# Last stage of a fused transformer kernel: a floor written as a reduction, a rotation in one instruction, and a new order of the pieces

## What is computed

```python
for i in range(6):
    x = attn_layer(shift_tokens(x), Wqkv[i], q_scale[i], k_scale[i], Wo[i]) + x
    x = ffn_layer(shift_tokens(x), ln_g[i], ln_b[i], W1[i], b1[i], W2[i], b2[i]) + x

def attn_layer(x, Wqkv, qs, ksc, Wo):          # 16 heads of 64
    q, k, v = jnp.split(x @ Wqkv, 3, -1)       # then split in heads
    q, k = l2norm(q) * qs, l2norm(k) * ksc     # l2norm: t / max(norm(t), 1e-12)
    q = q * cos * scale + rotate_half(q) * sin * scale
    k = k * cos / scale + rotate_half(k) * sin / scale
    out = local_attention(q, k, v)             # windows of 32, each sees itself and the one before, softmax
    return out @ Wo                            # heads joined again

def ffn_layer(x, g, bln, W1, b1, W2, b2):      # 341 wide
    a, gate = jnp.split((layernorm(x) * g + bln) @ W1 + b1, 2, -1)
    return a * gelu(gate) @ W2 + b2
```

## Time and profile before

| | us |
|---|---|
| median of 3 runs | 2295.93 |
| lowest and highest | 2290.71, 2298.35 |
| the profiled execution | 2290.53 |
| its span in the trace | 2288.7 |

### The profile page before, as it was taken

How to read it: one execution, slowest core, us unless ns; L and a number is a source line. 1 busy time by engine, 2 the same in 40 slices (tenths; PEclk the granted TensorE clock), 3 DMA queues, 4 the chain that set the end, 5 groups by cost and what they waited for, 6 DMA issues and landing times. The chain is left out here.

```text
span 2288.7 us, 52278 instructions
## 1 busy us (share of the span) xinstructions
PE 1844.2 (81%) x18512; PEld 917.1 (40%) x18512; DVE 1718.1 (75%) x3041; ACT 1279.6 (56%) x1850; POOL 922.8 (40%) x913
## 2 busy tenths in 40 slices
PE   5655888888888888888855888988988987988886
PEld 3531222222222222222222655655655655655554
DVE  4744777777677777777737988978988988987984
ACT  4411666656666666666644656655655655655653
POOL 0002111111111111111016877766776776775770
PEclk9955999999899999999978999999999999999998
DMA  1002223232323232322004333323332332332330
GB/s 34 1 17 62 54 57 61 57 60 56 60 56 60 56 60 56 60 56 57 2 3 130 94 95 94 95 87 89 93 94 76 95 105 76 95 105 67 95 85 10
DMA packets 88745, 152.83 MB, mean 67 GB/s; under 512 B 16819, under 2 KB 51669, under 8 KB 84693
## 3 DMA queue, kind: packets, MB, share of 16 engines
q1 hardware_dynamic: 86421, 149.04, 26.6%
q10 hardware_dynamic: 2112, 0.94, 0.2%
HBM read 98.03 MB, written 51.12 MB: 65 GB/s over the span
## 5 line engine op out<-in xcount | busy, mean ns | idle before, releaser
L899 DVE TENSOR_REDUCE ENM<-PM 128x1 f32<-128x512 f32 x1024 | 658.5, 686 | 249.9 <-PE PM L722 240.9
L819 ACT ACTIVATE EPT<-PA 128x1024 f32<-128x1024 f32 x512 | 512.3, 1021 | 219.3 <-PE PA L734 139.3
L722 PE MATMUL PM<-EKX,EQX 48*128 48x512 bf16 x1024 | 354.3, 399 | 103.1 <-DVE ENM L899 83.7
L1293 POOL TENSOR_TENSOR DRN<-DRN,DHALF 128x8 f32<-128x8 f32 x192 | 352.2, 1835 | 8.7
L1291 POOL TENSOR_TENSOR DQR<-DR 128x512 f32<-128x512 f32 x192 | 254.3, 1324 | 245.5 <-DVE DR L1581 221.2
L642 POOL CAST ENMP<-ENM 128x16 bf16<-128x16 f32 x64 | 12.7, 198 | 781.2 <-DVE ENM L899 781.2
L744 PE MATMUL PV<-EPT,EVP 128*32 128x512 f32 x2048 | 283.1, 626 | 0.9 <-ACT EPT L819 0.7
L722 PEld LDWEIGHTS PM<-EKX,EQX 48*128 48x128 bf16 x1024 | 85.5, 94 | 477.6 <-DVE ENM L899 392.5
L734 PE MATMUL PA<-EQX,EKX 51*128 51x512 bf16 x1024 | 253.2, 394 | 28.2 <-DMA EQX<-EROWS 14.2
L1337 PE MATMUL PM<-DWQKV,DXS 128*128 128x512 f32 x384 | 213.3, 638 | 38.3 <-ACT DRAW L1499 24.7
L1499 ACT ACTIVATE DRAW<-PM 128x512 f32<-128x512 f32 x192 | 114.9, 598 | 156.4 <-DVE DR L1581 93.1
(11 more groups left out here) (208 smaller groups left out, 2937.4 us busy)
## 6 DMA issues: line engine op xcount, KB each, us to landing
DV<-d_vpark SPq DMA_DIRECT2D x192, 256.0 KB, 5.1
d_vpark<-DVT SPq DMA_DIRECT2D x48, 512.0 KB, 2.6
e_park<-EPARTS SPq DMA_DIRECT2D x64, 192.0 KB, 2.9
EQX<-e_park SPq DMA_DIRECT2D x32, 384.0 KB, 5.4
EKX<-e_park SPq DMA_DIRECT2D x32, 384.0 KB, 9.1
DWQKV<-in_WqkvR SPq DMA_DIRECT2D x6, 1536.0 KB, 8.6
e_park<-EPARTS SPq DMA_DIRECT2D x64, 128.0 KB, 2.7
e_park<-EPARTS SPq DMA_DIRECT2D x64, 64.0 KB, 2.1
```

Source lines behind the costliest of these rows:

```text
L722: pe.matmul(PM[:, r, :], lhsT=QX[64 * r:64 * r + KQ, b, hp, t * 128:(t + 1) * 128], rhs=KX[64 * r:64 * r + KQ, b, hp, :], start=True, stop ...
L819: s_.activation(PT[:, kt, pair * 2 * S:(pair + 1) * 2 * S], PA[:, 2 * pair:2 * pair + 2, :].rearrange("p a b -> p (a b)"), ACT.Exp, scale= ...
L899: v.tensor_reduce(NM[:, g % 2, t, j, 0:1], PM[:, r, :], AX.X, ALU.max, negate=True).then_inc(maxed, 1)
L1293: g.tensor_tensor(rn, rn, HALF[:, 0:8], ALU.pow).then_inc(rooted.sem, 1)
```

## The change

- The floor: the sums get a second column that is set to 1e-24 once, and the floor becomes a maximum over the two columns with `tensor_reduce` in place of a `tensor_scalar`.
- The second product of the rotation is one `tensor_tensor` of 512 elements that reads the halves of each head in swapped order (a step of -1 over the two halves), in place of two of 256.
- The places are new. POOL's and SP's lists stay as they were. What changes in the lists (a prime marks a piece of the layer before):
  - DVE: `score` of tile n comes ahead of `weigh` of tile n-1, where it came behind it. `f1b` comes behind p1 (it came ahead of p0), `f1c` still between p2 and the next piece. The second `f3v` comes behind p1 (it came ahead of it). In round 8 `score` 7 and `weigh` 6 come behind `f4`, in the next turn of the loop, where they came ahead of the loop's end on either side of it.
  - PE: `f1b` comes behind p2 (it came right behind `f1a`, ahead of p1); the first `f3` ahead of `mix`; `score` 7 ahead of the loop's end, where it was the first piece of the loop.
  - ACT: `f1a` behind p0 in place of ahead of it; `exp` ahead of the third `f3`, where it came behind it: f33, f34, exp1, f35 in round 3 and f30, f31, exp6, f32 in round 8.

```diff
 TILE_PLACES = {
-    "score": {"tensor": (2, 4), "vector": (1, 48)},
-    "exp": {"scalar": (3, 2)},
-    "weigh": {"vector": (2, 45)},
-    "pturn": {"tensor": (3, 5), "scalar": (3, 7)},
-    "mix": {"tensor": (3, 25), "vector": (3, 17)},
-    "oturn": {"tensor": (3, 39), "scalar": (3, 32)},
-    "out": {"tensor": (3, 42), "vector": (3, 36)},
+    "score": {"tensor": (1, 49), "vector": (2, 0)},
+    "exp": {"scalar": (2, 44)},
+    "weigh": {"vector": (3, 8)},
+    "pturn": {"tensor": (3, 1), "scalar": (3, 8)},
+    "mix": {"tensor": (3, 28), "vector": (3, 12)},
+    "oturn": {"tensor": (3, 36), "scalar": (3, 35)},
+    "out": {"tensor": (3, 44), "vector": (3, 34)},
 }
 BATCH_PLACES = {
-    ("shift", None): {"tensor": (0, 4), "scalar": (0, 4), "gpsimd": (0, 4)},
-    ("f1a", None): {"tensor": (7, 12), "scalar": (7, 6)},
-    ("f1b", None): {"tensor": (7, 17), "vector": (7, 4), "gpsimd": (7, 26)},
-    ("f1c", None): {"vector": (7, 31.5)},
-    ("f2", None): {"tensor": (8, 14), "scalar": (8, 11)},
-    ("f3", 0): {"tensor": (8, 27), "scalar": (8, 26)},
-    ("f3", 1): {"tensor": (8, 37), "scalar": (8, 31)},
-    ("f3", 2): {"tensor": (8, 40.5), "scalar": (8, 45.5)},
-    ("f3v", 0): {"vector": (8, 0)},
-    ("f3v", 1): {"vector": (8, 20)},
-    ("f3v", 2): {"vector": (8, 34.5)},
-    ("f4", None): {"tensor": (8, 49), "vector": (8, 45)},
+    ("shift", None): {"tensor": (0, 0), "scalar": (0, 0), "gpsimd": (0, 0)},
+    ("f1a", None): {"tensor": (7, 11), "scalar": (7, 14)},
+    ("f1b", None): {"tensor": (7, 33), "vector": (7, 28), "gpsimd": (7, 26)},
+    ("f1c", None): {"vector": (7, 30.5)},
+    ("f2", None): {"tensor": (8, 13), "scalar": (8, 14)},
+    ("f3", 0): {"tensor": (8, 26), "scalar": (8, 23)},
+    ("f3", 1): {"tensor": (8, 35), "scalar": (8, 32)},
+    ("f3", 2): {"tensor": (8, 40.5), "scalar": (8, 44.5)},
+    ("f3v", 0): {"vector": (8, 9)},
+    ("f3v", 1): {"vector": (8, 23)},
+    ("f3v", 2): {"vector": (8, 30.5)},
+    ("f4", None): {"tensor": (8, 48), "vector": (8, 48)},
 }
...
-        SS, RN = m.sb("DSS", [128, 2, 8]), m.sb("DRN", [128, 2, 32])
+        SS, RN = m.sb("DSS", [128, 2, 8, 2]), m.sb("DRN", [128, 2, 32])
...
+                chain.link(v.memset(SS[:, :, :, 1], 1e-24))
...
-                        v.tensor_tensor(r2[:, :, 0:32], x[:, :, 32:64], bc(tab[:, 1, 0:32], 1, [128, 8, 32]), ALU.mult).then_inc(step, 1)
-                        v.tensor_tensor(r2[:, :, 32:64], x[:, :, 0:32], bc(tab[:, 1, 32:64], 1, [128, 8, 32]), ALU.mult).then_inc(rotated.sem, 1)
+                        halves = lambda y: y.rearrange("p h (s e) -> p h s e", s=2)
+                        v.tensor_tensor(halves(r2), halves(x)[:, :, ::-1, :], bc(tab[:, 1].rearrange("p (s e) -> p s e", s=2), 1, [128, 8, 2, 32]),
+                                        ALU.mult).then_inc(rotated.sem, 1)
                         wait(squared, k)
-                        v.tensor_reduce(SS[:, k % 2, :], SQ[:, k % 2, :].rearrange("p (h e) -> p h e", h=8), AX.X, ALU.add).then_inc(summed.sem, 1)
+                        v.tensor_reduce(SS[:, k % 2, :, 0], SQ[:, k % 2, :].rearrange("p (h e) -> p h e", h=8), AX.X, ALU.add).then_inc(summed.sem, 1)
                         wait(summed, k)
-                        v.tensor_scalar(RN[:, n[0] % 2, 8 * c:8 * c + 8], SS[:, k % 2, :], 1e-24, None, ALU.max).then_inc(floored.sem, 1)
+                        v.tensor_reduce(RN[:, n[0] % 2, 8 * c:8 * c + 8], SS[:, k % 2, :, :], AX.X, ALU.max).then_inc(floored.sem, 1)
```

## The result

The changed kernel takes 2286.45 us (median of 20 runs, 2276.71 to 2295.86), the kernel before 2299.21 us beside it (20 runs). The ratio is 0.9942, 95% interval 0.9924 to 0.996: 13 us faster, where 39 to 41 had been forecast. The profiled execution has a span of 2281.7 us, 7.0 less than before. What is read from traces is therefore always a stretch within the stack.

A forecast was written before the change was run, and what follows sets the result against it. DVE was taken to set the pace in the middle rounds, and chains in rounds 7 and 8. Terms -20 - 12.5 - 18 + 12 + 0 = -38.5 us gave 2252.0 or 2257.4, called 2255 us; range 2212 to 2292.

The forecast's parts named there:

- Middle rounds: Rounds 4 to 6 and two like them in the first layer: 1.0 us gained each, 20 us in all, bounds 6 and 38.
- Score ahead of weigh: DVE's swapped order in the middle rounds: costs nothing, as PE's score ends 1.4 us before DVE comes to it.
- the walk through the round: Middle round, piece by piece: floor gains kept 0.5 at p0, 0.1 p1, 0.2 p2, 0.3 to 0.5 p3, rotation 4 x 0.07.
- The floor: DVE's floor as a reduction: about 0.17 us, free of POOL's block, so DVE reaches its next instruction about 0.55 us sooner.
- POOL's work stays: POOL will be at its addition or multiplication in most of the time DVE gains; the block at p3 remains.
- The rotation: One product of 512 elements on DVE for two: 0.07 us saved a piece, or 0.55 lost if swapped reads ran half rate.
- Rounds 0 to 2: POOL is the next bound, f1c's wait goes: 2.5 us gained, five times, 12.5 us, bounds 0 and 25.
- Round 7: DVE's 1.04 us wait before f1c goes and three pieces shorten: 3.0 us gained, six times, 18 us, bounds 9 and 27.
- Round 3: ACT's exp and two loads before the third gelu, 3.62 us: 2.4 us lost, five times, 12 us, bounds 0 and 22.
- rival 3: Table switches delay the third gelu and PE's clock falls while it waits: slower, up to 6 us a place, 2308 us; chance 0.11.
- Round 8 and the loop's end: PE's f4 slips about 2.4 us, but the loop-end pauses are hidden: 0, six times, bounds 6 gained and 14 lost.
- Rival 1: POOL takes the gain: DVE's wait at the floor moves to L1579; 12 us gained in all, 2281 us; chance 0.22.

The follow-up runs named there:

- its own kernel: The kernel before with only the second product of the rotation put in one instruction: 2307.36 us against 2310.31, ratio 0.9991.
- f1 places alone: The kernel before with only the new places of f1a and f1b: 2289.79 us, ratio 0.9943.
- forms alone: The kernel before with the new instructions (floor as a reduction, rotation in one) and the old places: 2288.93 us, ratio 0.9949.
- places alone: The kernel before with all the new places and the old instructions: 2313.95 us, ratio 1.0067.
- exp behind: The kernel after, but with exp on ACT behind the third gelu again: 2258.11 us, ratio to the kernel before 0.9821.

## Why the prediction was wrong, point by point

The way was right, the size was not: 13 us gained in place of 39 to 41. The measured 2286.45 us lie within the range that the rivals had widened to 2212 to 2292, and outside the forecast's own bounds of 2228 to 2278.

- **Middle rounds.** 1.0 us each forecast, 1.2 measured, but the nearness is partly luck. The forms, from which all of the 1.0 was to come, gave 0.7 alone. Score ahead of weigh was said to cost nothing and was given no gain; it is 0.5 us a round. The floor fell to 0.17 us without spread, and p2 and p3 stay blocked, as the walk through the round had it.
- **The floor.** The step "POOL's work stays" held: 37% of the freed time returned at the first product.
- **The rotation.** 0.07 us a piece was forecast and no difference was measured; its own kernel won 0.5 us in three middle rounds and lost 1.3 in round 2.
- **Rounds 0 to 2.** 2.5 us forecast. 0.8 were gained from the first product to the first score, and 1.6 in round 2 when the `weigh` that left it is counted: 2.4. The 1.5 of the f1 places alone say the same of round 2.
- **Round 7.** 3.0 forecast and measured. The reason held as far as the traces go: a wait gone and shorter pieces. `f1c`'s wait for POOL is gone with the places (idle 2.8 us in all ahead of it, 14.2 before) and not with the forms alone (16.4). With the forms alone round 7 takes 24.2 us in the mean (23.0 in two of the four layers), with the places alone 24.4, and with both 21.9: it takes both. How the 3.0 us divide into the two was not measured apart from the clock, which differs between these traces.
- **Round 3: the term that was mis-sized.** 2.4 us forecast, 4.6 measured, 4.2 of it gone with exp behind. The parts were named: load, exp and load 3.66 us, `f3v` late, 1.3 us for the score. What was left out of the sum is the clock: PE, idle for 2.6 us, took 4.48 to 5.49 us for `f4` in all five layers, and not the 2.94 of before, 2.0 us more in the mean. The prediction has this in rival 3 and not in the forecast.
- **Round 8 and the loop's end: the step that failed.** I let a slip of 2.4 us and a hidden pause at the loop's end cancel. The slip was about right: `f4` starts 3.0 us later after its score when the moved `weigh` is taken off, and 2.2 of that go with exp behind. The pause was not hidden: the stretch from `f4` to the next layer's first product took 15.15 us before and 15.09 after, where 2.4 gained had been forecast. On DVE the pause is 3.28 us and on PE 4.39, against 1.97 and two of 1.5 to 2.3, and moving PE's score to either side of the branch changes nothing (0.9804 against 0.9821).
- **The sum.** A layer was to gain 6.1 us and gained 1.5: 2.2 are missing in round 3, 3.0 in rounds 8 to 2 (0.5 lost where 2.5 gained had been forecast), and 0.6 more came in the middle rounds. Over the kernel, with 5, 5 and 6 layers, that turns -38.5 into about -16; -13 were measured. The kernel with exp behind takes 2258 us, which is 3 us from the forecast, but by luck: the prediction's own terms give it -38.5 - 12 - 14.4 = -65 us, and 41 were measured. What it lacks lies around the loop's end again: rounds 8 to 2 take 73.8 us in it, 1.3 gained where 4.9 would have been.

Rival 1 has the nearest number, 12 us gained, and it is luck too: it wanted 0.3 us from a middle round and nothing from rounds 0 to 2, and 37% of the freed time came back where it had nearly all. Rival 3 had the right mechanism and the wrong price: 4.6 us a place was its point of decision, 6 its price, and 2.5 and 3.2 were measured. By the Trainium skill (ScalarE: Activation LUTs, Table sets) one does all functions of one set and then all of the other. The runs bear the rule out: breaking it cost 35 us in the kernel before and 28 in the kernel after. The 2.7 us that it gives for a switch are not seen here: in the kernel after the next function starts 1.29 to 1.30 us after the load's start in 45 of its 46 loads.

## What to carry to other kernels

Of a list of places that was moved as a whole, check first what each engine's own state makes of the new neighbours: here two half-steps of a place put exp between two gelus, and that took two thirds of all that the change had gained. Price such a switch at the loads plus the work between them plus what the matrix engine loses in clock while it waits, and do not set a hidden pause against it that no row shows as hidden. An instruction form that keeps DVE from meeting POOL at the SBUF pays for what is left of it behind the next instruction that does meet POOL, so look at form and order together: alone the forms gained 12 us and the places lost 15, together they gained 13.

## What the runs showed of the hardware

- A floor of 8 elements as `tensor_scalar` took 171 to 845 ns beside POOL's work, as `tensor_reduce` over 16 elements 169 to 171 ns in the same 192 places.
- A read with a step of -1 over halves of 32 elements runs at the speed of a plain one: 683 ns against 692 for the other product, medians.
- At the end of a hardware loop PE stands for 4.4 to 4.8 us when 256 short instructions (128 matmuls of 64x64 with their weight loads) stand right ahead of the branch, and for two pauses of 1.5 to 2.3 us when they stand behind it. DVE stands for 3.3 to 3.5 us in the kernel after and for 1.9 to 2.0 in the kernel before. What the pauses are made of was not tried.
- PE that had waited 2.6 us did the next 24 matmuls in 4.48 to 5.49 us in round 3 of the kernel after, five times of five; after 2.6 to 2.8 us of waiting it did them in 2.92 to 2.94 us in four of six times in its round 8, and in 5.49 in the other two. After 0.4 to 0.5 us of waiting, before, it was 2.92 to 2.94 each time. The granted clock was 0.79 of full over most of a slow one that took 4.49 us, 0.51 over one of 5.49, and 1.00 over the whole of a round 8 with a quick one. Why round 3 is slow each time and round 8 is not was not tried.
